# Four layers of a graph network on one core: the last chunk of the last layer in two halves, and the row moments of three chunks by ScalarE

## The reference

```python
h = maximum(layernorm(x), 0)              # rows of 256, eps 1e-5, no weights
def sage(h, Wl, Wr, b):
    mean = segment_sum(h[src], dst) / maximum(degree, 1)
    return mean @ Wl + h @ Wr + b
h = relu(sage(h, Wl1, Wr1, b1))           # 256 -> 256
h = relu(sage(h, Wl2, Wr2, b2))           # 256 -> 128
h = relu(sage(h, Wl3, Wr3, b3))           # 128 -> 256
return x + sage(h, Wl4, Wr4, b4)          # 256 -> 256
```

## Time and profile before

| | us |
|---|---|
| median of three runs | 710.55 (707.74 to 710.88) |
| the profiled execution, its own time | 705.95 |
| its span, first to last instruction | 704.2 |
| TensorE busy | 661.6 (94%) |
| VectorE busy | 292.0 (41%) |
| ScalarE busy | 172.2 (24%) |
| GpSimd busy | 31.4 (4%) |
| granted TensorE clock, mean | 0.981 |

### The profile page before, as it was taken

One profiled execution on the slowest core, in us unless ns is written; L12 is line 12 of the kernel. 1 busy time (PEld: TensorE's weight loads), 2 busy tenths in 40 slices (PEclk: granted clock), 3 DMA queues, 4 the chain that ended last, 5 costly groups with the idle time before them and its releaser, 6 DMA issues.

```text
span 704.2 us, 11350 instructions
## 1 busy us (share of the span) xinstructions
PE 661.6 (94%) x4499; PEld 364.3 (52%) x4500; DVE 292.0 (41%) x826; ACT 172.2 (24%) x339; POOL 31.4 (4%) x80
## 2 busy tenths in 40 slices
PE   5568998899999999999999999999999999999996
PEld 4234555655555465554444444544444646556454
DVE  6898776487775776840112222222221110101001
ACT  4844664363551540311001001121120000000000
POOL 8000000000000000000000000000001010110110
PEclk9999999898999999999999999999999999999999
DMA  8000020410100100126242313021122033031130
GB/s 265 26 5 1 1 93 2 171 35 7 44 19 19 62 16 4 61 18 74 83 135 71 116 60 104 34 94 60 60 62 104 19 97 105 1 105 50 55 104 31
DMA packets 35536, 43.52 MB, mean 62 GB/s; under 512 B 8138, under 2 KB 20958, under 8 KB 35488
## 3 DMA queue, kind: packets, MB, share of 16 engines
q1 hardware_dynamic: 35372, 42.62, 20.5%
q10 hardware_dynamic: 116, 0.24, 0.1%
HBM read 26.73 MB, written 15.79 MB: 60 GB/s over the span
## 4 chain that ended last, share of the span: by engine, by line
PE 88%; DVE 6%; ACT 3%; issue 2%; POOL 1%; DVEq 0%; POOLq 0%; ACTq 0%
PE agg_ps L1790 33%; PE window_ps L1790 21%; PE lin_ps L1706 6%; PE window_ps L1662 6%; PE lin_ps L1730 6%; PE lin_ps L1747 5%; PE lin_ps L1810 3%; DVE early L1194 2%; PE lin_ps L1755 2%; PE turn_ps L1772 2%; ACT counts L1434 1%; PE degree_ps L1822 1%; PE degree_ps L1593 1%; PE turn_ps L1593 1%; PE degree_ps L1586 1%
## 5 line engine op out<-in xcount | busy, mean ns | idle before, releaser
L1790 PE MATMUL agg_ps<-counts,H 128*128 128x512 f16 (+3 forms) x1026 | 241.4, 362 | 0.0
L1194 DVE TENSOR_TENSOR early<-early 128x512 f16<-128x512 bf16 (+2 forms) x466 | 153.6, 389 | 40.0 <-PE window_ps L1662 38.7
L1434 ACT ACTIVATE counts<-window_ps 128x400 f16<-128x400 f32 x196 | 96.1, 504 | 136.4 <-PE window_ps L1662 132.4
L1662 PEld LDWEIGHTS window_ps<-early 128*128 128x128 f16 x892 | 70.5, 101 | 113.6 <-issue 32.0
L1662 PE MATMUL window_ps<-early 128*128 128x100 f16 (+1 forms) x892 | 101.0, 224 | 24.2 <-DVE early L1194 13.9
L1790 PEld LDWEIGHTS agg_ps<-counts,H 128*128 128x128 f16 (+1 forms) x1026 | 81.1, 99 | 53.8 <-issue 8.7
L1790 PE MATMUL window_ps<-counts,early 128*128 128x512 f16 (+2 forms) x396 | 89.0, 379 | 0.0
L1790 PE MATMUL window_ps<-counts,H 128*128 (+3 forms) x339 | 66.6, 351 | 0.0
L1790 PEld LDWEIGHTS window_ps<-counts,early 128*128 128x128 f16 (+1 forms) x396 | 38.4, 98 | 46.7 <-issue 3.4
L1790 PEld LDWEIGHTS window_ps<-counts,H 128*128 128x128 f16 (+1 forms) x339 | 29.3, 97 | 33.9 <-issue 1.5
L1790 PE MATMUL agg_ps<-counts,early 128*128 (+3 forms) x297 | 46.9, 314 | 0.0
(11 more groups left out here) (170 smaller groups left out, 448.3 us busy)
## 6 DMA issues: line engine op xcount, KB each, us to landing
selfT<-hT_d SPq DMA_DIRECT2D x18, 512.0 KB, 4.2
hT_d<-newT SPq DMA_DIRECT2D x12, 512.0 KB, 4.1
rdeg<-rdeg_d SPq DMA_DIRECT2D x18, 256.0 KB, 4.2
counts<-in_x_dram SPq DMA_DIRECT2D x6, 512.0 KB, 8.0
hT_d<-counts SPq DMA_DIRECT2D x6, 512.0 KB, 3.2
newH<-in_x_dram SPq DMA_DIRECT2D x6, 512.0 KB
out_dram<-newT SPq DMA_DIRECT2D x6, 512.0 KB
hT_d<-newT SPq DMA_DIRECT2D x6, 256.0 KB, 4.0
```

The lines of the kernel that those rows point to most:

```text
L1194: last = v.tensor_tensor(hot[:, group % GROUPS, 0:n * size].rearrange("p (r n d) -> p r n d", r=n, d=2), numbers_to[:, 0:size].rearrange(" ...
L1434: a.activation(counts[:, :, 2 * w * WIN:2 * (w + 1) * WIN].rearrange("p t (a w) -> p a t w", a=2), window_ps[:, FILL_AT[w] % 2, 0:2 * KEYS ...
L1662: m(window_ps[:, at % 2, key0:key0 + keys], hot_src[:, group % GROUPS, r * P:(r + 1) * P], hot_key[:, group % GROUPS, r * keys:(r + 1) * k ...
L1790: last = m((agg_ps, window_ps)[bank][:, h, 0:n], tile[:, part, h * P:(h + 1) * P], counts[0:rows_, k, chunk_cols(c, n)], start=first and p ...
```

## The change

It has two parts.

**Layer 4, last chunk.** TensorE's loop over the places ends two places earlier; place 5 is written out, and the last chunk's sums are made for two halves of 256 nodes (`add_half`), each over all 25 tiles, in the two banks. The linear part of place 5 comes after tile k = 8 of the first half. The linear part of the last chunk (`last_lin`) goes into four places in PSUM, one for each node tile: for node tiles 0 and 1 after k = 6 of the second half, for tiles 2 and 3 the selfT products after k = 20 and the aggT products after the second half, h by h. VectorE scales each half when it is summed (`scale_half`) and adds x4 tile by tile (`add_last`); SyncE stores the four tiles with a DMA each.

**Moments.** For places 4, 5 and 6, VectorE's `h0_moments` is gone. ScalarE does a Copy scaled by -1/256 with a running sum, giving minus the mean, and a Square with that as bias and a running sum, giving 256 times the variance, for each tile of rows: `h0_moment(j, i)`. It does those of place 4 between windows 22 and 29 of the first fill, those of places 5 and 6 in the first round. Each of the two is waited for before ScalarE goes on. The square root's scale and the shift's sign follow from that.

The semaphores and the buffer `spare` are declared; the rest of the diff is:

```diff
-        def over_places(eng, do, first):
+        def over_places(eng, do, first, places=NCH):
             do(1, 1 - first)
             do(2, first)
-            with eng.Fori(1, NCH // 2) as i:
+            with eng.Fori(1, (places - 1) // 2) as i:
...
+        def last_ps(i):
+            return (lin_ps[:, 0, 0:D], lin_ps[:, 1, 0:D], degree_ps[:, 0:D], turn_bank[:, 0:D])[i]
+        ON_ACT = 4
...
+                    if last and l == 4:
+                        for i in range(TPC):
+                            sp.wait_ge(rows_made[i], 1)
+                            c = ORDER[-1]
+                            sp.dma_start(out[c * CH + i * P:c * CH + (i + 1) * P, :],
+                                         newT[:, :, :].rearrange("p a b -> p (a b)")[:, i * D:(i + 1) * D]
+                                         ).then_inc(last_stored, 16)
+                        return
...
-            first_round = {0: lambda: (h0_shift(3), below(), degrees(0)), 1: lambda: h0_moments(4),
-                           4: lambda: (h0_low_part(3), h0_shift(4)), 6: square_weights, 7: lambda: choose_late(2, 0),
-                           8: lambda: (h0_moments(5), h0_low_part(4)), 9: lambda: choose_late(2, 1),
+            first_round = {0: lambda: (h0_shift(3), below(), degrees(0)), 4: lambda: (h0_low_part(3), h0_shift(4)), 6: square_weights, 7: lambda: choose_late(2, 0),
+                           8: lambda: h0_low_part(4), 9: lambda: choose_late(2, 1),
                            10: lambda: choose_late(2, 2), 11: lambda: (h0_shift(5), choose_late(2, 3)),
-                           12: lambda: h0_moments(6), 13: lambda: choose_late(3, 0),
+                           13: lambda: choose_late(3, 0),
...
+            def scale_half(bank, g):
+                cols = slice(g * HALF_CH, (g + 1) * HALF_CH)
+                for h in range(2):
+                    dve.wait_ge(agg_done[4], 2 * (NCH - 1) + 2 * g + h + 1)
+                    v.scalar_tensor_tensor(out=aggT[:, h, cols], in0=(agg_ps, window_ps)[bank][:, h, cols],
+                                           scalar=unscale[:, 3:4], in1=rdeg[:, cols], op0=ALU.mult, op1=ALU.mult
+                                           ).then_inc(agg_scaled[4], 1)
+            def add_last(i):
+                dve.wait_ge(last_products[i], 4)
+                rows_out = newT[:, :, :].rearrange("p a b -> p (a b)")[:, i * D:(i + 1) * D]
+                v.tensor_tensor(rows_out, last_ps(i), x4[:, i, :], ALU.add).then_inc(rows_made[i], 1)
+            dve.wait_ge(rdeg_loaded[4], 16 * NCH)
+            dve.wait_ge(lin_done[4], both(NCH - 1, 2, 1))
+            scale_half(FIRST_BANK[4], 0)
+            dve.wait_ge(x4_biased, both(NCH, TPC, 1))
+            dve.wait_ge(out_stored, 16 * (NCH - 1))
+            add_last(0)
+            add_last(1)
+            scale_half(1 - FIRST_BANK[4], 1)
+            add_last(2)
+            add_last(3)
...
+            def h0_moment(j, i):
+                c = ORDER[j]
+                if i == 0:
+                    act.wait_ge(x_loaded[c], 16)
+                order.after(a.activation(spare, x_in[c][:, i, :], ACT.Copy, scale=-1.0 / D,
+                                         accum_out=moments[c][:, i, 0:1]))
+                ins = a.activation(spare, x_in[c][:, i, :], ACT.Square, bias=moments[c][:, i, 0:1],
+                                   accum_out=moments[c][:, i, 1:2])
+                order.after(ins)
...
-                       20: lambda: h0_high_part(2), 31: lambda: h0_root(3)}
+                       20: lambda: h0_high_part(2), 22: lambda: h0_moment(4, 0), 24: lambda: h0_moment(4, 1),
+                       26: lambda: h0_moment(4, 2), 28: lambda: h0_moment(4, 3), 31: lambda: h0_root(3)}
...
+            first_round = {0: lambda: h0_whole(3), 1: lambda: h0_moment(5, 0), 2: lambda: (h0_root(4), first_rows(3, slice(0, MID),
                                                                                       degree_ps[:, 0:MID])),
+                           3: lambda: h0_moment(5, 1), 4: lambda: h0_relu(4, (0, 1)),
+                           5: lambda: (h0_relu(4, (2, 3)), h0_moment(5, 2)), 6: lambda: h0_high_part(4),
+                           7: lambda: h0_moment(5, 3), 8: lambda: h0_moment(6, 0),
+                           9: lambda: (h0_root(5), h0_moment(6, 1)), 10: lambda: (norms(0), norms(1)),
+                           11: lambda: (norms(2), h0_relu(5, (0, 1))), 12: lambda: (h0_relu(5, (2, 3)), h0_moment(6, 2)),
+                           13: lambda: (h0_high_part(5), h0_moment(6, 3), h0_root(6)), 14: lambda: late_sources(2),
...
+            def add_half(bank, k, g):
+                cols = slice(g * HALF_CH, (g + 1) * HALF_CH)
+                c = ORDER[-1]
+                rows_, parts = (STACK, 1) if k == NT - 1 else (P, 2)
+                tile = H_tiles(4, k, 1)[0:rows_, 0, :, :]
+                for h in range(2):
+                    for part in range(parts):
+                        last = m((agg_ps, window_ps)[bank][:, h, cols], tile[:, part, h * P:(h + 1) * P],
+                                 counts[0:rows_, k, c * CH + g * HALF_CH:c * CH + (g + 1) * HALF_CH],
+                                 start=k == 0 and part == 0, stop=k == NT - 1)
+                    if k == NT - 1:
+                        last.then_inc(agg_done[4], 1)
+            def last_lin(i, k, of):
+                node = slice(i * P, (i + 1) * P)
+                m(last_ps(i), (aggT, selfT)[of][:, k, node], W14[:, of, k, :], start=of == 1 and k == 0,
+                  stop=of == 0 and k == 1).then_inc(last_products[i], 1)
...
-                over_places(pe, place, FIRST_BANK[l])
-            lin(4, NCH - 1)
+                if l < 4:
+                    over_places(pe, place, FIRST_BANK[l])
+            over_places(pe, place, FIRST_BANK[4], NCH - 2)
+            place(NCH - 2, 0 if FIRST_BANK[4] else 1)
+            bank = FIRST_BANK[4]
+            pe.wait_ge(agg_scaled[4], 2 * (NCH - 2))
+            for k in range(NT):
+                add_half(bank, k, 0)
+                if k == 8:
+                    lin(4, NCH - 2)
+            pe.wait_ge(agg_scaled[4], 2 * (NCH - 1))
+            for k in range(NT):
+                add_half(1 - bank, k, 1)
+                if k == 6:
+                    pe.wait_ge(self_loaded[4], 16 * NCH)
+                    pe.wait_ge(out_made, both(NCH - 1, 2, 1))
+                    for i in range(2):
+                        for j in range(2):
+                            last_lin(i, j, 1)
+                    pe.wait_ge(agg_scaled[4], 2 * NCH)
+                    for i in range(2):
+                        for j in range(2):
+                            last_lin(i, j, 0)
+                if k == 20:
+                    for i in range(2, 4):
+                        for j in range(2):
+                            last_lin(i, j, 1)
+            for j in range(2):
+                pe.wait_ge(agg_scaled[4], 2 * NCH + j + 1)
+                for i in range(2, 4):
+                    last_lin(i, j, 0)
```

More of the change, by code:

```diff
@@ L397, in sage_stack_kernel @@
         moments = [nook(TPC, 2) for _ in range(NCH)]
+        spare = nook(D // 2).bitcast(f16)
         eps = nook(1)
@@ L499, in sage_stack_kernel @@
         x4_biased = sem("x4_biased")
+        last_products = [sem(f"last_products_{i}") for i in range(TPC)]
         out_made = sem("out_made")
+        rows_made = [sem(f"rows_made_{i}") for i in range(TPC)]
         out_stored = sem("out_stored")
+        last_stored = sem("last_stored")
         AGG = [0, 2, 1, 1, 2]
@@ L793, in _ @@
                 after(NCH - 1, last=True)
-            sp.wait_ge(out_stored, 16 * NCH)
+            sp.wait_ge(out_stored, 16 * (NCH - 1))
+            sp.wait_ge(last_stored, 16 * TPC)
         @block.gpsimd
@@ L958, in h0_shift @@
                 order.after(v.reciprocal(rstd[:, c, 0:t], rstd[:, c, 0:t]))
-                v.scalar_tensor_tensor(out=shift[:, c, 0:t], in0=moments[c][:, 0:t, 0], scalar=-1.0,
+                v.scalar_tensor_tensor(out=shift[:, c, 0:t], in0=moments[c][:, 0:t, 0], scalar=-1.0 if j < ON_ACT else 1.0,
                                        in1=rstd[:, c, 0:t], op0=ALU.mult, op1=ALU.mult).then_inc(shift_made, 1)
@@ L1370, in _ @@
                     place(0, FIRST_BANK[l])
-                    over_places(dve, place, FIRST_BANK[l])
+                    over_places(dve, place, FIRST_BANK[l], NCH - 2)
+                    place(NCH - 2, 1 - FIRST_BANK[l])
+            def scale_half(bank, g):
[19 more added lines that the diff above has]
+            add_last(3)
         @block.scalar
@@ L1388, in h0_root @@
                 n, t = size_of(c)
-                act.wait_ge(moments_made, BEFORE[j + 1])
+                if j < ON_ACT:
+                    act.wait_ge(moments_made, BEFORE[j + 1])
                 a.activation(rstd[:, c, 0:t], moments[c][:, 0:t, 1], ACT.Sqrt, bias=eps[:, 0:1],
-                             scale=H0_SCALE ** -2).then_inc(root_made, 1)
```

(3 more changed lines are left out.)

6 lines of the change are left out of this document (1 added, 5 removed).

## The result

The changed kernel takes 705.04 us, the median of 20 runs (703.2 to 706.64). The kernel before took 709.69 us in 20 runs beside it (705.66 to 711.79). The prediction was 710.2, with 706.9 as its low end.

What follows compares the result with a forecast made beforehand. TensorE, busy 661.6 of 704.2 us, was taken as the bound, with time to gain only in its stops at start and end. Tail -1.3 and moments +0.9 gave -0.4 us: 705.6 profiled, 710.2 median, range 706.9 to 713.4.

Steps and rivals of the forecast that it cites:

- the clock: Low-clock stretch from 66.8 to 69.6 us, after TensorE's long stop: left as it is, no gain or loss counted.
- the base: Starting time: the profiled execution's 705.95 us, called quick by 4.6 against the 710.55 median of three runs.
- The last chunk in halves: End of layer 4: 6.8 us less after the last scaling, 5.2 and 0.3 back in matmuls, net -1.3 us.
- the store: Last store, 128 KB instead of 512 KB: gain between 0 and 1.0 us, taken as 0.4.
- the other case: Matmuls of 256 columns at some 98 ns by the skill's weight-load figures: the halves would gain 2 us.
- The moments, replayed: ScalarE's twelve rows in first fill and first round, 1.25 us each: two delays, +0.9 us in sum (+0.2 to +2.0).
- The second delay: Stores near 59.18 us come 1.95 us later behind place 5's rows; VectorE catches up 1.73, leaving +0.2 us.
- The prediction's last sign: An early part ahead of before would mean that the two delays on ScalarE aren't real; no size given.
- Rival B: Nearly free sums on ScalarE, clock staying at 2.4 GHz, tail at -2.2: -3.4 us, 707.2 us; chance 0.17.
- C: First round bound by ScalarE, window stores waiting behind rows of moments: +2.4 us, 713.0 us, or 714.4; chance 0.15.
- D: Last chunk's 256-column matmuls don't cover their weight loads, 0.13 us instead of 0.11: +4, 714 us; chance 0.06.
- E: ScalarE reloads tables between Square and Sqrt: +3.8 us, 713.9 us, or 718 by the skill's figure; chance 0.04.

Runs made afterwards that it cites:

- E1: Kernel before with the first part of the change alone (last chunk in halves, moments still on VectorE): 706.54 us, 0.996.
- E4: The whole changed kernel, measured again on the same chip as its parts: 705.96 us, 0.9943.
- E3: E1 with the last chunk's four additions all waited for and one store of 512 KB in place of four: 709.07 us, 0.9987.
- E10: Kernel before, last chunk whole and matmul order unchanged, with its additions and stores tile by tile: 708.55 us, 0.9982.
- E15: E2's kernel profiled again, one execution: span 703.4 us.
- E2: Kernel before with the second part of the change alone (moments of places 4, 5, 6 on ScalarE): 707.1 us, 0.9956.
- E8: Changed kernel with ScalarE's last row of place 4, place 4's root and all rows of place 5 moved to k = 1: 703.56 us, 0.9929.
- E12: Kernel before with VectorE's moments of place 5 moved from k = 8 to k = 1, none on ScalarE: 706.07 us, 0.9956.
- E11: E8's front with E9's end: 700.75 us, 0.9902.
- E13: E12's front with E9's end: 702.07 us, 0.9908.
- E7: Kernel before with ScalarE's twelve rows added, VectorE still doing its own moments into unread memory: 710.74 us, 1.0021.
- E9: Kernel before, last chunk whole, its selfT products ahead of its aggT products, additions and stores by tile: 706.14 us, 0.9955.
- E5: Kernel before with the moments of place 4 alone on ScalarE: 707.98 us, 0.9993.
- E6: Kernel before with the moments of places 5 and 6 alone on ScalarE: 706.76 us, 0.9975.

## Why the prediction was wrong

It said no difference, and the kernel is 0.6% faster. The measured median is 5.2 us under the predicted one. Of that the clock, a term put at nothing, is some 1.4 us, the base 0.9, the end 0.8 and the moments themselves 0.4; 1.7 us stay open. Point by point:

**The last chunk in halves: -2.1 us, predicted -1.3 with ends at -2.2 and -0.5.** All profiles with this tail agree (38.74 and 38.75 us in E1, E4 and the changed kernel, against 40.83 or 40.84). The scaling of 256 took 0.48 to 0.50 (predicted 0.48), the last addition 0.42 (0.42), the loads were covered. The matmuls of 256 columns took 0.109 us (predicted 0.108 to 0.112), so the 196 cost some 0.1 (0.3). The mis-sized term is the store, "the gain lies between 0 and 1.0; I take 0.4": E3 puts it at 1.24, outside both ends, and SyncE's wait shows 1.1 of it. The row nearest to it was the right one: the loads of selfT landed 1.4 us sooner at half the size. E10 shows besides that 1.43 of the 2.1 us come from additions and stores by tile, without any halves.

The Trainium skill ("TensorE: Matmul & The Clock Gate", Back-to-back issue gap) gives N/2.4 + 2.5 ns for a warm matmul by itself, 109 for 256 columns, and the row above has 0.109. Its figure for streams with weight loads, from which the prediction had some 98 ns as the other case, this trace doesn't bear out, though each of these matmuls has a weight load. Nothing hangs on it.

**The moments, replayed: nearly right.** A row costs 1.18 us (predicted 1.25): 0.41 + 0.51 for the two activations and 0.39 for the two reads, overlapped a little. Round 0 started 0.5 later (predicted 0.7): from the first window at 14 to 15 us to its first matmul it is 30.6 us in every profile with place 4's moments on VectorE and 31.1 in every one with ScalarE's four rows in the first fill. The second delay was predicted at +0.2; without a low stretch round 0 is as long with the rows as without (60.7 in E15, E2 and E1, in the table above). TensorE's new stop and the shorter one of VectorE came where they were expected. At an unchanged clock the part costs some 0.5, predicted 0.9. The prediction's last sign, that an early part ahead of before would mean that the two delays aren't real, fails too: round 0 is shorter on the mean, and both delays are in the trace.

**The clock: this step failed.** The prediction put it as "I leave that as it is; the stop only moves to the front". It did not stay as it was. With the 2.68 us stop of before, a stretch at the 1.2 GHz level begins at 65.6 to 67.4 us in 6 of 7 profiles with an unchanged front, within 0.8 us of the moment when TensorE has work again. In the changed kernel and E4 it begins at 65.5 and 64.8, and the slower work takes the place of a later stop; in E2 and E15 it is absent. By the last column of the table the unchanged fronts have a mean of 62.2 and the changed ones (changed, E4, E2, E15) one of 60.8: -1.4 us in a term that was put at nothing. The idle time is the same: 0.55 + 2.68 before, 1.69 + 0.56 + 0.97 in E15, 3.2 us in both. E1, which has the long stop but no low stretch, has a round 0 as long as theirs by the last column. So what counted was what the low clock fell on, with one long stop made into shorter ones. Rival B had this term and its size ("the 2.83 us at half clock would be 1.4"), and "its better end" for the tail, -2.2, was nearly what came; only its nearly free sums were wrong. With the moments early (E8, E12) 1.7 us of idle time go as well, which is 60.7 - 59.0, and the low stretch is absent in all four profiles with that front (E8, E11, E12, E13).

That the gain comes by VectorE's relief is shown by E7 (taken away: 1.0021 against 0.9956) and E12 (the relief alone, without ScalarE: 0.9956). That it works through the clock is shown by the equal idle time and the table of round 0, and the mean clocks of all runs agree: E2's mean clock is 0.0026 higher than that of before, 1.8 us of the 2.4 by which its mean span is shorter. What decides whether a given execution gets the low stretch was not tried by itself.

**The base.** The sum was made against an execution with a span of 704.2 when the kernel's mean is 707.3, and carried to the median of three runs. Over 20 runs that median is 709.69, not 710.55: 0.9 of the 5.2 us. Places 1 to 6 of layer 1 took 197.60 us in that execution and 199.22 to 201.40 in the six other profiles with an unchanged front, since it had 20.5 us at the low level there and they had 23.9 to 30.7. Among the 95 runs of before, the 18 with a mean clock of 0.981, as the profiled one had, have a mean span of 704.2, the 57 with 0.976 one of 707.8. Measured against it, the changed kernel's profile shows its gain cancelled.

**The rivals.** C's sum takes the tail at -1.0 where the text has -1.3; with that it is 712.7 and not 713.0. C is real as a mechanism: TensorE's 1.70 us are put down to ScalarE, and E7, which has its delays without the relief, is 1.5 us slower (0 to 3.0). It is outweighed. D falls with 0.109 us, E with two table loads in all: Square and Sqrt alternate here without a reload.

**Do the terms add up?** The pieces of the profiles (the end's length; the start, +0.5 where ScalarE has all the rows of place 4 in the first fill; the last column of the table) against what the ratios say on 709.7:

| us | pieces | ratio |
|---|---|---|
| E1, tail | -2.1 | -2.8 (-4.0 to -1.7) |
| E9, selfT first | -3.1 | -3.2 (-4.7 to -1.6) |
| E10, stores by tile | -1.4 | -1.3 (-2.8 to 0.1) |
| E3, halves with one store | -0.9 | -0.9 (-2.5 to 0.6) |
| E5, place 4 alone | +0.5 + 0.1 = +0.6 | -0.5 (-2.4 to 1.5) |
| E6, places 5 and 6 | -1.5 | -1.8 (-3.4 to -0.2) |
| E7, moments twice | +0.5 + 1.9 = +2.4 | +1.5 (0.0 to 3.0) |
| E8 | -3.2 - 2.1 = -5.3 | -5.0 (-7.4 to -2.8) |
| E12 | -3.2 | -3.1 (-4.7 to -1.6) |
| E11 | -3.2 - 3.1 = -6.3 | -7.0 (-9.2 to -4.7) |
| E13 | -3.2 - 3.1 = -6.3 | -6.5 (-9.0 to -4.1) |
| E2, moments | +0.5 - 1.4 = -0.9 | -3.1 (-4.2 to -2.0) |
| the change | -2.1 - 0.9 = -3.0 | -4.2 (-5.3 to -3.1) |

**Open.** The last two rows miss about 1 to 2 us. By the ratios the parts alone make -2.8 - 3.1 = -5.9, by the pieces -3.0, and the whole change has -4.2 (E4: 0.9943, the same); the intervals of the parts leave room for that, so E1 and E2 may each have come out somewhat high. Places 1 to 6 of layer 1 may hold a part: they took 199.4 us on the mean of the changed kernel, E4, E2 and E15, and 200.4 on that of the seven with an unchanged front. But single profiles there lie between 197.1 and 201.6 in all versions, by how long the low stretches near 110, 133 and 175 us last, and what sets those lengths was not found. From four and seven profiles that 1.0 us is not shown.

## What to carry to other kernels

A stop of TensorE has a second price, the stretch at 1.2 GHz that may follow it on real work: of two schedules with the same idle time, the one with shorter stops can win, and work of another engine that stands in front of the longest stop should go where that engine waits anyway before it is given to a third. At the end of a kernel, store in small pieces as they come, and keep products that need no late operand for the time in which the late one is made. Before summing sub-percent effects against one profiled execution, look at how its clock record and span stand among other executions.

## What the runs showed of the hardware

- A last store of 128 KB ended the kernel 1.24 us sooner than one of 512 KB (E1 and E3); the wait for its landing was 1.4 against 2.5 us.
- An activation with a running sum adds a separate read of the accumulator of 0.19 to 0.20 us; the Copy of 128x256 took 0.41 us, as without a sum (0.42), the Square 0.51.
- The low clock behind one and the same 2.68 us stop lasted 3.4 us, 6.8 us or came not at all, in executions of the same front; it cost 1.5, 3.0 and 0 us. One of 3.4 us that began between shorter stops cost 0.2, since a later wait went with it. TensorE's first rise to full clock varied from 6.0 to 9.2 us after the start of round 0, and each microsecond of it cost a half; up to it, where the record reaches back, the granted clock was 0.50 and 512 columns took 0.42 us.
- Among 95 runs of one kernel the span goes with the mean granted clock: 704.2 us at 0.981, 707.8 at 0.976, 709.1 at 0.974.
